# Two transposes of quantised tiles and one copy move to other places of a loop

## The reference

```
x = x + conv_ref(ln_c(x), fc1_w, fc2_w, sa_w)     # channel gate, then 7x7 spatial gate
t = to_tokens(x)
t = t + ffn_ref(ln_t(t), w1, w2)
# conv_ref: ca = sigmoid(mlp(mean(x)) + mlp(max(x))); x = x * ca
#           s = conv7x7([mean_c(x), max_c(x)]);       x * sigmoid(s)
# ffn_ref:  h = bitlinear(x, w1); h = gelu(h); bitlinear(h, w2)
# bitlinear: rows of x rounded to 127 steps of their largest magnitude, w rounded to -1, 0, 1 (times its rms)
```

## Time and profile before

| | |
|---|---|
| median of 3 runs | 291.68 us (291.13 to 291.74) |
| profiled execution | 290.93 us, of which the span is 289.2 us |
| PE busy | 256.5 us (89%) |
| DVE, ACT, POOL busy | 230.0, 229.0 and 159.8 us |
| granted TensorE clock, mean | 0.975 of full speed |

### The profile page before, as it was taken

How to read it: one execution, slowest core, us unless ns; L and a number is a source line. 1 busy time by engine, 2 the same in 40 slices (tenths; PEclk the granted TensorE clock), 3 DMA queues, 4 the chain that set the end, 5 groups by cost and what they waited for, 6 DMA issues and landing times.

```text
span 289.2 us, 5900 instructions
## 1 busy us (share of the span) xinstructions
PE 256.5 (89%) x1842; PEld 153.2 (53%) x1850; DVE 230.0 (80%) x535; ACT 229.0 (79%) x467; POOL 159.8 (55%) x265
## 2 busy tenths in 40 slices
PE   1655948976899999999999999999999999999995
PEld 1434734644446565656565656565656555544544
DVE  0573778999888898889888988898889887998531
ACT  0775779895887889788978897889798977898541
POOL 8414863233774487448744874487448743376330
PEclk9999975998999999999999999999999999999999
DMA  7999700000334235633562356235603550373757
GB/s 190 389 384 423 228 24 2 1 0 2 73 76 106 77 75 123 140 105 75 125 166 75 73 129 157 82 74 128 131 3 72 130 126 20 57 181 73 124 98 215
DMA packets 71622, 34.20 MB, mean 118 GB/s; under 512 B 52584, under 2 KB 68968, under 8 KB 71080
## 3 DMA queue, kind: packets, MB, share of 16 engines
q1 hardware_dynamic: 69844, 32.78, 44.4%
q10 hardware_dynamic: 1748, 1.05, 1.3%
HBM read 14.94 MB, written 6.29 MB: 73 GB/s over the span
## 4 chain that ended last, share of the span: by engine, by line
PE 68%; DVE 9%; ACT 8%; issue 6%; POOL 2%; DMA 2%; ACTq 2%; another core or an unknown queue 1%; POOLq 0%; DVEq 0%; SPq 0%
PE ps_o L1299 22%; PE ps_h L1286 12%; PE ps_t L1286 12%; PE front L1214 4%; PE front L1204 3%; PE front L1329 3%; PE small L1260 3%; PE small L1230 2%; DMA hq<-w_raw 2%; PE front L1269 2%; PE small L1224 1%; ACT junk_p L578 1%; ACTq L345 1%; DVE amax L946 1%; ACT junk L578 1%
## 5 line engine op out<-in xcount | busy, mean ns | idle before, releaser
L1299 PE MATMUL ps_o<-w2T,hq 128*128 128x512 f16 x352 | 85.2, 379 | 0.8 <-DMA hq<-w_raw 0.8
L515 POOL TENSOR_SCALAR w_room<-w_room,q 128x1024 f32<-128x1024 f32 x48 | 53.6, 1127 | 23.7 <-DVE q L956 23.0
L946 DVE TENSOR_REDUCE amax<-w_room 128x1 f32<-128x1024 f32 (+1 forms) x48 | 57.9, 1206 | 6.5 <-ACT w_room L578 6.5
L1286 PE MATMUL ps_h<-w1T,xq 128*128 128x512 f16 x208 | 53.1, 393 | 0.7 <-ACT xq L578 0.7
L578 ACT ACTIVATE w_raw<-w_room 128x1024 f16<-128x1024 f16 x46 | 48.4, 1055 | 4.3 <-POOL w_room L515 3.5
L1299 PEld LDWEIGHTS ps_o<-w2T,hq 128*128 128x128 f16 x352 | 33.5, 98 | 32.4 <-DMA hq<-w_raw 1.3
L1286 PE MATMUL ps_t<-w1T,xq 128*128 128x512 f16 x176 | 42.6, 379 | 0.0
L578 ACT ACTIVATE w_room<-ps_h,s 128x512 f32<-128x512 f32 x52 | 35.5, 685 | 6.6 <-PE ps_h L1286 5.8
L578 ACT ACTIVATE w_room<-ps_t,s 128x512 f32<-128x512 f32 x44 | 29.6, 690 | 6.4 <-PE ps_t L1286 6.2
L1286 PEld LDWEIGHTS ps_h<-w1T,xq 128*128 128x128 f16 x208 | 19.9, 102 | 20.1 <-issue 2.7
L504 POOL TENSOR_SCALAR cen<-cen,q 128x512 f32<-128x512 f32 x24 | 16.7, 695 | 21.2 <-DVE q L938 21.2
(11 more groups left out here) (136 smaller groups left out, 470.1 us busy)
## 6 DMA issues: line engine op xcount, KB each, us to landing
out<-w_room SPq DMA_DIRECT2D x15, 384.0 KB, 3.4
x_in<-in_x SPq DMA_DIRECT2D x14, 384.0 KB, 4.1
w_room<-in_L_ffn_w SPq DMA_DIRECT2D x4, 1024.0 KB, 8.8
w_raw<-in_L_ffn_w SPq DMA_DIRECT2D x4, 1024.0 KB, 11.7
x_in<-in_x ACTq DMA_DIRECT2D x2, 384.0 KB, 3.9
hq<-w_raw SPq DMA_TRANSPOSE x48, 3.1
out<-w_room SPq DMA_DIRECT2D x3, 128.0 KB, 1.9
fc_raw<-in_L_conv_fc_w ACTq DMA_DIRECT2D x2, 128.0 KB, 4.4
```

Source lines behind the costliest of these rows:

```text
L515: pool.tensor_scalar(part, part, q2[tile.par][:, 0:1], MAGIC, ALU.mult, ALU.add).then_inc(g_rounded, 1)
L946: chain.mark(dve.tensor_reduce(amax2[:, i:i + 1], w1_room[:, first + i * F // 2:first + (i + 1) * F // 2 + i], AX.X, ALU.max, apply_absolu ...
L1286: last = pe.matmul(banks[b], xq[tile.pair.par][:, tile.s, k, :], w1T[:, k, b * 512:(b + 1) * 512], start=(k == 0), stop=(k == NC - 1))
L1299: last = pe.matmul(out_bank(tile)[:, :], hq[tile.par][:, k, :], w2T[:, k, :], start=(k == 0), stop=(k == NF - 1))
```

## The change

PE, in the loop body: the last quarter of `ffn_out` of tile 0 is cut in two halves of two matmuls, and `turn_xq` of the next pair's tile 0 stands between them instead of ahead of the quarter. `turn_xq` of tile 1 stands behind the fourth quarter of `ffn_out` of tile 1 instead of ahead of it. `fc2` stands behind both `turn_x`, instead of between them. ACT, in the loop body: `copy_out` of tile 1 and the channel sum of tile 2 now stand ahead of `pack_g(Tile(nxt, 0), 0)`, and `copy_out` ahead of that sum.

```diff
@@ ACT, body
                 if attend:
                     sum_channels(Tile(att, 0))
                     sum_channels(Tile(att, 1))
+                copy_out(Tile(pair, 1), OUT_BANK[2])
+                if attend:
+                    sum_channels(Tile(att, 2))
                 if normalise:
                     pack_g(Tile(nxt, 0), 0)
-                if attend:
-                    sum_channels(Tile(att, 2))
-                copy_out(Tile(pair, 1), OUT_BANK[2])
                 if turn:
                     copy_x(Tile(fresh, 2), X_BANK[2])
@@ PE
-            def ffn_out(tile, quarters):
+            def ffn_out(tile, quarters, parts=(0, 1)):
                 for i in quarters:
+                    first, last_k = i * NF // 4 + parts[0] * NF // 8, i * NF // 4 + (parts[-1] + 1) * NF // 8
...
-                    for k in range(i * NF // 4, (i + 1) * NF // 4):
+                    for k in range(first, last_k):
...
-                    if i == 3:
+                    if last_k == NF:
                         last.then_inc(o_done, 1)
@@ PE, body
                 ffn_out(Tile(pair, 0), (2,))
+                ffn_out(Tile(pair, 0), (3,), (0,))
                 if normalise:
                     b = turn_xq(Tile(nxt, 0), XQ_BANK[0], b)
-                ffn_out(Tile(pair, 0), (3,))
+                ffn_out(Tile(pair, 0), (3,), (1,))
...
-                ffn_out(Tile(pair, 1), (2,))
+                ffn_out(Tile(pair, 1), (2, 3))
                 if normalise:
                     b = turn_xq(Tile(nxt, 1), XQ_BANK[1], b)
                 if attend:
                     fc1(att)
-                ffn_out(Tile(pair, 1), (3,))
-                if attend:
                     if turn:
                         a = turn_x(Tile(fresh, 0), X_BANK[0], a)
+                        b = turn_x(Tile(fresh, 1), X_BANK[1], b)
                     fc2(att)
-                    if turn:
-                        b = turn_x(Tile(fresh, 1), X_BANK[1], b)
```

## The result

| | before | after |
|---|---|---|
| median | 291.71 us (291.13 to 291.95, 6 runs) | 293.9 us (293.69 to 294.68, 6 runs) |
| profiled execution, span | 290.93, 289.2 us | 294.34, 292.6 us |
| PE busy | 256.5 us | 259.2 us |
| mean granted clock | 0.975 | 0.977 |

The ratio is 1.0077 (95% interval 1.0058 to 1.0095): the change costs 2.2 us. A second series gave 294.1 against 291.78 us, ratio 1.0089 (1.0069 to 1.0110). The forecast was 293.5 with a range of 292.3 to 294.8. The direction and the mechanism were right, with one term of the sum, the gap ahead of `fc1`, mis-sized. The size, +1.83 us, was 0.4 us short of the first series and about 0.8 short of the 2.61 that the two traces show in the loop.

What follows compares the result with a forecast made beforehand. PE was taken to bound the loop, a pass being its list plus its stalls. Pass 0 -0.23, passes 1 to 4 +0.80, pass 5 +0.33, pass 6 +0.93 gave +1.83 on 291.68: 293.5 us, range 292.3 to 294.8.

Steps and rivals of the forecast that it cites:

- the gap ahead of `fc1`: PE, tile 1, passes 0 to 5: 0.22 us, taken as a wait for ACT's mean that goes; `fc1` starts 0.64 later.
- Chain A: From PE's `turn_xq` through ACT's copy to `ffn_in`: 1.08 us that PE's own work must cover.
- The stall of 0.10: Tile 0, passes 1 to 5: PE work of 0.98 over a copy chain of 1.08, so 0.10 us lost per pass.
- those of 0.43 and 0.86 in pass 6: PE's stalls at tile 0 and tile 1 of pass 6, where only 0.65 and 0.22 us cover the copy.
- Rival 2: The 0.22 ahead of `fc1` is PE's own and stays in six passes: +3.15 us, 294.8; chance 0.11.
- Chain B: From `fc1` through DVE's list to `turn_ca`: 3.45 us; PE's work over it falls from 3.99 to 3.12, `turn_ca` at -0.54.
- Rival 1: No wait at `turn_ca` in passes 0 to 4, `fc1` to `turn_ca` below 3.2 us: not slower, 291.4; chance 0.11.
- -0.33: Pass 0, tile 0: two matmuls fill part of PE's wait for POOL at `turn_xq`; gain 0.33 us.
- fc2: PE, tile 1: its wait for `hidden` is covered in full passes; about 0.5 us in pass 5, costing nothing more.
- ACT's order: Earlier `copy_out` gains 0.41 us in pass 5 and 0.23 in pass 6, none in full passes; later `pack_g` costs 0.
- Rival 3: Clock falls in PE's unbroken row of transposes and small matmuls: +1.7 us in each of six passes, 304; chance 0.04.

Runs made afterwards that it cites:

- e5: The changed kernel with `fc1` ahead of tile 1's `turn_xq`; median 295.43 us, one execution.
- e4: The changed kernel with both `turn_xq` of pass 6 back where they stood before; median 294.05 us, ratio 1.0079 to before.
- e1: The kernel before with ACT's new order alone; median 291.11 us, ratio 0.9983 to before.
- e6: The changed kernel with DVE's `split_gate` ahead of the second `hidden_max` of tile 0; median 294.76 us, ratio 1.0108 to before.
- e3: The kernel before with only tile 1's `turn_xq` behind the fourth quarter and `fc2` behind both `turn_x`; median 294.46 us, ratio 1.0102 to before.
- e2: The kernel before with only tile 0's `turn_xq` between the halves of the last quarter; median 291.84 us, ratio 1.0013 to before.
- e7: Before plus ACT's new order, tile 0's split in pass 0 alone, `fc1` between tile 1's last-quarter halves in passes 0 to 4; 290.41 us, ratio 0.9955 to before.
- e10: e7 with two of `fc1`'s three waits moved earlier in PE's list; median 290.52 us, ratio 0.9962 to before.
- after_again: The changed kernel run once more, unchanged; median 294.1 us, ratio 1.0089 to before.

## Why the prediction was right, and where it was short

*Chain A*, 1.08: right. It was 1.07 to 1.09 in after (82.67 behind `turn_xq` at 81.58 in pass 0) and 1.17 for the `turn_x` of e5. The stall of 0.10 in passes 1 to 5 and those of 0.43 and 0.86 in pass 6 came as forecast, and e4 took pass 6 back to 22.96, where e1 has 22.97.

*The gap ahead of fc1*: the term that was mis-sized. "PE goes on 0.10 later, so 0.22 is a wait for it": I took the whole gap for the wait, and it was 0.12 wait and 0.10 of `fc1`'s own. Rival 2 had the right idea with the wrong share. `fc1` moved by 0.86 - 0.12 = +0.74 and not by +0.64. The row was readable: the mean ended 0.10 before `fc1` started, and I took that 0.10 for the time in which a semaphore releases PE. It stayed when the mean was 0.94 early.

*Chain B*, 3.45: 3.48 in full passes and in pass 5 (236.74 to 240.22). It was DVE's list that decided, as argued, and e6 shows it. `turn_ca` gained 0.51 by standing closer, not 0.54. Rival 1, B below 3.2, is refuted.

With both terms put right, the steps give -0.33 + 0.74 - 0.51 = -0.10 for pass 0 (measured -0.09), 0.10 + 0.74 - 0.51 = +0.33 for passes 1 to 4 (+0.34), 0.10 + 0.74 + 0.03 - 0.41 = +0.46 for pass 5 (+0.45) and, unchanged, +0.93 for pass 6 (+0.89). The sum is 2.61, which the loop shows. The two errors, 0.10 and 0.03 in each of six passes, are the 0.8 that were missing. For pass 0 the agreement to 0.01 is in part luck, since the moment at which POOL releases its first `turn_xq` moves by up to 0.19 between traces. So is it that the forecast lies within 0.4 of the measured median: the medians differ by 2.2 and 2.3 in the two series, a little less than the loops.

*fc2*: right. In pass 5 it waited 0.43 inside B, in full passes not at all. But such a wait may not be free: at it and that of `turn_ca` the clock fell in e3 and e4, which the prediction had not priced.

*ACT's order*: -0.41 and -0.23 forecast, -0.41 and -0.21 alone in e1. `ffn_out` waited for `hq` nowhere in the loop but ahead of its first matmul, where the start decides.

*Rival 3*, the clock in the new row of 2.6 us: it stayed at 1.00 in every full pass. The rule of the Trainium skill ("TensorE: Matmul & The Clock Gate", Part 4: PE-mode transpose), by which transposes do not count as a busy PE the way matmuls do, did not bring the clock down here. Where it did fall, it was at the second of two idle times of PE.

## What to carry to other kernels

In a pass that one engine fills, count what stands over each chain of other engines before moving its start: four matmuls (0.86) taken from over a chain of 3.45 with 0.54 to spare cost more than the wait that they removed. Stalls on one engine don't add: one ahead of a wait is swallowed by it, so a part tried alone can look free and cost its full size beside the others. A gain ahead of a wait is swallowed in the same way, as pass 0 of e2 and e7 shows. And of a gap between two instructions only that part is a wait which ends with the releaser; check on another place of the same instruction, where the releaser is long done, how much gap remains.

## What the runs showed that I had not expected

`fc1` (fp32, 64 columns of weights) starts about 0.10 us later than the instruction ahead of it allows: 0.10 in after, 0.08 in e5, 0.10 in e7 and 0.09 in e10, behind transposes and behind large matmuls, with three waits at it or with one.

The clock went to 0.50 in the second of two waits of 0.43 and 0.48 us, 2.4 us apart, or right behind it, in the traces of e3 and e4, and stayed at 1.00 behind the same two waits in those of after and after_again. When it fell it cost 1.5 and 1.7 us, more than both waits together.

The time to the first `ffn_out` differs by 1.2 us between executions of one kernel (76.72 and 77.96 in before), while its loop repeats to 0.1 (192.86 and 192.95). Medians of three runs see this scatter; of the pass lengths of one trace only that of pass 0 sees some of it.
